# Attention in a hybrid block: queries loaded by tile, head loads spread, and one more quarter turned by DMA

## The reference, cut to what matters

```python
qf = jnp.transpose(qn.reshape(b, g, cq, h * w), (0, 1, 3, 2))
kf = jnp.transpose(key_.reshape(b, g, cq, h * w), (0, 1, 3, 2))
vf = jnp.transpose(value.reshape(b, g, cq, h * w), (0, 1, 3, 2))
scores = jnp.einsum('bgnc,bgmc->bgnm', qf, kf) * (1.0 / math.sqrt(c))
attn = jax.nn.softmax(scores, axis=-1)
ctx = jnp.einsum('bgnm,bgmc->bgnc', attn, vf)
```

## Time and profile before

| | |
|---|---|
| median of 3 runs | 8012.96 us |
| the profiled execution | 7983.15 us, span 7981.2 us |
| TensorE (PE), matmuls | 6932.5 us busy, 87% |
| VectorE (DVE) | 5846.9 us, 73% |
| GpSimd (POOL) | 5711.2 us, 72% |
| ScalarE (ACT) | 4440.0 us, 56% |
| DMA transposes `lo_turned<-p_lo`, issued by SP | 1024, 3.1 us from issue to landing (median) |
| loads of a head, issued by ScalarE | `q_head` 2 x 1024 KB, `k_head` 2 x 512 KB, `v` 1024 KB |
| store of a head, issued by ScalarE | `attn_out` 1024 KB |

### The profile page before, as it was taken

How to read it: one execution, slowest core, us unless ns; L and a number is a source line. 1 busy time by engine, 2 the same in 40 slices (tenths; PEclk the granted TensorE clock), 3 DMA queues, 4 the chain that set the end, 5 groups by cost and what they waited for, 6 DMA issues and landing times. The chain is left out here.

```text
span 7981.2 us, 140152 instructions
## 1 busy us (share of the span) xinstructions
PE 6932.5 (87%) x43076; PEld 4111.4 (52%) x43076; DVE 5846.9 (73%) x8015; ACT 4440.0 (56%) x7219; POOL 5711.2 (72%) x2792
## 2 busy tenths in 40 slices
PE   8798999899899759999999999999999986858992
PEld 6565666666566523443443444344444433536882
DVE  4486777787678648999899989989989996640116
ACT  2376777777677536656656665666566552212223
POOL 0187787787788529999999999999999995331006
PEclk9899999999999879999999999999999998978995
DMA  3467767767767641111211211121121112342113
GB/s 107 120 123 129 136 122 135 137 121 137 130 122 128 166 137 69 67 54 66 72 51 67 72 67 55 66 73 50 66 72 67 55 64 78 135 154 74 58 56 130
DMA packets 1256926, 755.82 MB, mean 95 GB/s; under 512 B 1113238, under 2 KB 1151796, under 8 KB 1235504
## 3 DMA queue, kind: packets, MB, share of 16 engines
q1 hardware_dynamic: 1233360, 677.46, 33.4%
q10 hardware_dynamic: 17120, 58.83, 2.9%
q0 software_dynamic: 6144, 16.33, 0.6%
HBM read 360.72 MB, written 123.73 MB: 61 GB/s over the span
## 5 line engine op out<-in xcount | busy, mean ns | idle before, releaser
L1492 DVE TENSOR_TENSOR_SCAN hh<-mb_ps_da,state,hh 128x512 f32<-128x512 f32 x2048 | 2496.0, 1273 | 126.4 <-POOL hh L1405 73.9
L1405 POOL TENSOR_TENSOR hh<-dtx,bb 128x1024 f32<-128x1024 f32 x1024 | 2399.6, 2369 | 214.6 <-PE mb_ps_y L1154 210.3
L661 POOL TENSOR_TENSOR p_lo<-prob 128x1024 bf16<-128x1024 f32 x1024 | 1906.8, 1893 | 803.1 <-ACT prob L612 664.6
L1295 ACT ACTIVATE mb_ps_da<-dt,amat 128x512 f32<-128x512 f32 x2048 | 1391.6, 686 | 1336.2 <-DVE hh L1492 1329.6
L1154 PE MATMUL mb_ps_y<-hh,ident 128*128 128x512 f32 x4096 | 1971.3, 609 | 17.4 <-POOL hh L1411 12.0
L676 DVE TENSOR_SCALAR_CACHE_REDUCE prob<-ps_s 128x1024 f32<-128x1024 f32 x1024 | 1213.8, 1223 | 487.5 <-PE ps_s L543 487.4
L1154 PEld LDWEIGHTS mb_ps_y<-hh,ident 128*128 128x128 f32 x4096 | 790.1, 195 | 962.5 <-issue 855.2
L612 ACT ACTIVATE prob<-prob,nmx 128x1024 f32<-128x1024 f32 x1024 | 1163.6, 1138 | 53.8 <-issue 19.5
L1499 DVE TENSOR_TENSOR hh<-hh,mb_ps_c 128x1024 f32<-128x1024 f32 x768 | 927.9, 1208 | 248.7 <-PE mb_ps_c L1143 214.6
L543 PE MATMUL ps_s<-k_head,q_tile 64*128 64x512 f32 x4096 | 1030.5, 622 | 46.2 <-ACT q_tile L648 45.8
L567 PE MATMUL ps_o<-v,hi_turned 128*128 128x128 bf16 x8192 | 841.0, 221 | 140.0 <-DMA lo_turned<-p_lo 138.6
(11 more groups left out here) (222 smaller groups left out, 8103.6 us busy)
## 6 DMA issues: line engine op xcount, KB each, us to landing
bb<-mb_bc SPq DMA_DIRECT2D x128, 1024.0 KB, 4.6
cc<-mb_bc SPq DMA_DIRECT2D x256, 256.0 KB, 3.1
lo_turned<-p_lo SPq DMA_TRANSPOSE x1024, 3.1
mb_u<-u SPq DMA_DIRECT2D x32, 512.0 KB, 3.2
m_dirs<-mo SPq DMA_DIRECT2D x32, 512.0 KB, 8.3
ex_w<-in_L_ffn_w SPq DMA_DIRECT2D x16, 1024.0 KB, 7.5
q_head<-q_full ACTq DMA_DIRECT2D x12, 1024.0 KB, 19.3
xbuf<-ml_zero SPq DMA_DIRECT2D x16, 640.0 KB, 5.5
```

The lines of the kernel that those rows point to most:

```text
L661: pool.tensor_tensor(lo[:, c, :], prob[s.u][:, cs], hi_view[s.u][:, 2 * c * PW + 1:2 * (c + 1) * PW:2], ALU.subtract).then_inc(lo_ready, 1)
L1295: act.activation(ps_da[:, exp_bank(e), :], dt[:, j, blk, :], ACT.Exp, scale=amat[:, j, blk, r % S:r % S + 1]).then_inc(da_ready, 1)
L1405: pool.tensor_tensor(hh[:, r % RING], dtx[:, j, half(r // S)], bb[:, r % S, :].unsqueeze(1).broadcast_to([P, HK, CH]), ALU.mult).then_inc( ...
L1492: dve.tensor_tensor_scan(h, a, h, state[:, s.j, q % S, blk:blk + 1], ALU.mult, ALU.add).then_inc(scanned, 1)
```

## The change

Four things change in attention.

1. Queries are no longer loaded a head at a time. SP loads the 128 queries of a tile straight from `q_full` into `q_tile`, in two loads of 64 rows x 512 bytes (32 KB), two tiles ahead. ScalarE's copy is gone.
2. The loads of keys and values are cut in halves and issued by ScalarE one at a time: keys in tiles 0 and 1, values in tiles 3 and 30; the store of the head before stands in tile 2. For that, tiles 0 to 3, 30 and 31 are written out.
3. Piece 3 of the upper halves is no longer turned by TensorE. ScalarE packs it into `p_hi` (128 x 1024 bfloat16), and SP issues a fifth DMA transpose for it, between those of pieces 1 and 2 of the lower halves.
4. Of the three pieces that are left, ScalarE evicts 1 and VectorE 0 and 2; the two PSUM buffers alternate over three pieces a tile.

Semaphores are split accordingly (`k_loaded`, `v_loaded`, `q_loaded`, `hi_ready`, `hi_turned`). The first scores wait for the keys and queries of head 0 alone, the first product of each head for its values.

The diff, cut to its core:

```diff
-    qf = [sb(f"q_head{j}", [P, L]) for j in range(2)]
+    hi = sb("p_hi", [P, PW], BF16)
...
-    ON_ACT, ON_DVE = (1, 2), (0, 3)
+    ON_ACT, ON_DVE, CROSSED = (1,), (0, 2), 3
...
         step(Tile(h, j, hp, 0, 0, opening, closing, first=True))
-        step(Tile(h, j, hp, 1, 1, opening, closing))
-        with eng.Fori(1, QT // 2 - 1) as it:
+        for t in range(1, 4):
+            step(Tile(h, j, hp, t, t % 2, opening, closing))
+        with eng.Fori(2, QT // 2 - 1) as it:
...
-        if k in ON_ACT:
+        if k == CROSSED:
+            eng.wait_ge(hi_turned, ONE + (g + 1) * 16)
+        elif k in ON_ACT:
...
+    def load_k(eng, h, j, half):
+        part = slice(DH * half, DH * half + DH)
+        eng.dma_start(kf[j][part], k_full[ds(h * DH, DH), :].rearrange("d (c two n) -> d two c n", two=2, n=CH)[:, half]).then_inc(k_loaded[j], 16)
+
+    def load_v(eng, h, j, half):
+        part = slice(half * QT // 2, (half + 1) * QT // 2)
+        eng.dma_start(vv[j][:, part, :].rearrange("p t c -> p (t c)"),
+                      v_split[h, :, half * L // 2:(half + 1) * L // 2]).then_inc(v_loaded[j], 16)
+
+    def load_q(eng, h, t, u):
         for half in range(2):
+            eng.dma_start(qcur[u][DH * half:DH * half + DH, :], q_full[ds(h * DH, DH), ds(t * P, P)]).then_inc(q_loaded[u], 16)
...
         def _(sp):
             def step(s):
+                if s.q_after:
+                    sp.wait_ge(s_ready, ONE + (s.g + 1) * PAIR)
+                    stand(sp, stood)
+                    load_q(sp, s.h + 1 if s.q_next_head else s.h, s.u if s.q_next_head else s.t + 2, s.u)
                 for c in range(PIECES):
...
                     sp.dma_start_transpose(lo_t[:, s.u, c], lo[:, c, :]).then_inc(lo_turned[c], 16)
+                    if c == 1:
+                        sp.wait_ge(pv_done, ONE + s.g * PIECES + 2 * PIECES)
+                        stand(sp, stood)
+                        sp.wait_ge(hi_ready, ONE + s.g + 1)
+                        stand(sp, stood)
+                        sp.dma_start_transpose(hi_t[:, CROSSED, :].rearrange("p (m c) -> p m c", c=P), hi[:, :]).then_inc(hi_turned, 16)
...
                 for k in range(PIECES):
-                    transposes(s, k)
+                    if k != CROSSED:
+                        transposes(s, k)
...
+            def pack(s):
+                act.wait_ge(exp_ready, ONE + (s.g + 1) * PIECES)
+                act.wait_ge(hi_turned, ONE + s.g * 16)
+                act.activation(hi[:, :], hi_view[s.u][:, 2 * CROSSED * PW + 1::2], ACT.Copy).then_inc(hi_ready, 1)
 
             def step(s):
                 exps(s.g, s.u, 3)
-                if s.q_after:
-                    tile_of(s)
                 turn(s, 1)
-                turn(s, 2)
+                pack(s)
...
-                if s.store_before:
-                    store(act, s.h - 1, 1 - s.j)
-                if s.load_after:
-                    load(act, s.h + 1, 1 - s.j)
+                if s.static and not s.opening:
+                    if s.t < 2 and not s.closing:
+                        load_k(act, s.h + 1, 1 - s.j, s.t)
+                    if s.t == 2:
+                        store(act, s.h - 1, 1 - s.j)
+                    if s.t == 3 and not s.closing:
+                        load_v(act, s.h + 1, 1 - s.j, 0)
+                    if s.t == QT - 2 and not s.closing:
+                        load_v(act, s.h + 1, 1 - s.j, 1)
```

More of the change, by code:

```diff
@@ L464, in attention_phase, with __init__ @@
     class Tile:
-        def __init__(s, h, j, hp, t, u, opening, closing, first=False, last=False):
+        def __init__(s, h, j, hp, t, u, opening, closing, first=False, last=False, pair=None):
             s.h, s.j, s.hp, s.t, s.u = h, j, hp, t, u
             s.g = h * QT + t
+            s.g2 = h * (QT // 2) + (t // 2 if pair is None else pair)
             s.before, s.after = not (first and opening), not (last and closing)
@@ L530, in step @@
                     sp.dma_start_transpose(lo_t[:, s.u, c], lo[:, c, :]).then_inc(lo_turned[c], 16)
-            load(sp, 0, 0)
-            load(sp, 1, 1)
+                    if c == 1:
[4 more added lines that the diff above has]
+                        sp.dma_start_transpose(hi_t[:, CROSSED, :].rearrange("p (m c) -> p m c", c=P), hi[:, :]).then_inc(hi_turned, 16)
+            load_q(sp, 0, 0, 0)
+            load_k(sp, 0, 0, 0)
+            load_k(sp, 0, 0, 1)
+            load_q(sp, 0, 1, 1)
+            load_v(sp, 0, 0, 0)
+            load_v(sp, 0, 0, 1)
+            for half in range(2):
+                load_k(sp, 1, 1, half)
+                load_v(sp, 1, 1, half)
             heads(sp, step)
@@ L548, in transposes, with values @@
                 pe.wait_ge(exp_ready, ONE + s.g * PIECES + k + 1)
-                turned(pe, s.g, k - 2)
+                slot = (s.u + k) % 2
+                if k == 2:
+                    turned(pe, s.g, 0)
+                else:
+                    turned(pe, s.g - 1, k + 1)
                 for m in range(BLOCKS):
                     at = 2 * (k * PW + m * P)
-                    last = pe.transpose(ps_t[:, k % 2, m * P:(m + 1) * P], hi_view[s.u][:, at + 1:at + 2 * P:2], ident16[:, :])
+                    last = pe.transpose(ps_t[:, slot, m * P:(m + 1) * P], hi_view[s.u][:, at + 1:at + 2 * P:2], ident16[:, :])
                 last.then_inc(t_ready, 1)
-            def values(hi=None, low=None):
+            def values(hi=None, low=None, first=False, hp=0):
                 if hi:
@@ L559, in values @@
                     turned(pe, g, k)
+                    if k == 0 and first:
+                        pe.wait_ge(v_loaded[j], ONE + (hp + 1) * 32)
                     if k == 0:
@@ L575, in step @@
                 for k in range(PIECES):
-                    transposes(s, k)
+                    if k != CROSSED:
+                        transposes(s, k)
                     if k >= LAG:
                         low = (s.g, s.u, s.j, k - LAG - 1) if k > LAG else (s.g - 1, 1 - s.u, s.jb, PIECES - 1) if s.before else None
-                        values((s.g, s.u, s.j, k - LAG), low)
+                        values((s.g, s.u, s.j, k - LAG), low, s.static and s.t == 0, s.hp)
                     elif s.before:
@@ L709, in step @@
                     maximum(s.g + 1, 1 - s.u)
-                turn(s, 3)
+                turn(s, 2)
                 if s.before:
```

54 lines of the change are left out of this document (19 added, 35 removed).

## The result

The changed kernel takes **8147.24 us** (median, 8140.28 to 8148.33) where the kernel before, measured beside it, takes 8012.81: a ratio of 1.0168, 95% interval 1.0151 to 1.0186. It is slower by 134 us. The forecast said slower by 43 us, 8056. Its sign and its bound were right, the size was a third of what came. The range held the time by 3 us (7915 to 8150), and the forecast's own ends, 7990 to 8145, missed it by 2.

What follows compares the result with a forecast made beforehand. SP's issue queue was to bound attention at 9.26 us a tile: +6 for tiles, +49 for head loads, -12 at the start, +43 us in sum, giving 8056 us against the median 8012.96; range 7915 to 8150.

Steps and rivals of the forecast that it cites:

- the forecast's own ends: Span of the main case, SP as the bound, from its terms' lower and upper ends: 7990 to 8145 us, chance 0.56.
- The bound: In attention, SP's issue queue becomes the bound at 9.26 us a tile, against 8.09 for TensorE and 7.45 for GpSimd.
- TensorE's part: In each attention tile TensorE loses eight transposes, 0.46 us, and alone would need 8.09 us instead of 8.55.
- ScalarE and VectorE, no term: Per tile the two swap similar work, staying near 6.8 and 6.9 us busy, so nothing was added to the forecast.
- SP's sum of 9.26 us a tile: SP's queue per tile: 6.26 today, 1.54 fifth transpose, 0.29 and 0.10 gaps, 1.07 two query loads; +6 us in all.
- 24 tiles with constant numbers, 0.8 us less each: Six tiles outside the loop in each of heads 0, 1, 6 and 7 have shorter gaps on SP, 0.8 us less each.
- Loads of a head, +49: At head changes, key and value loads and stores stretch SP's issues: 19 MB at 2.6 us each, +49 us.
- Start, -12: At attention's start, first scores need only four issues and two key loads, so begin earlier: -12 us (-5 to -18).
- The DMA engines keep up: In each tile, five transposes take 6.8 us of the DMA engines' time, out of 9.26, so they do not bound.
- TensorE stays the bound: Rival: SP's queue hides gaps and issues, its attention tile stays below 8.09 us; -238 us, 7775 us; chance 0.10.
- Cheap loads: Rival: each query load holds SP only 0.32 us, so SP needs 8.83 us a tile; 7946 us; chance 0.22.
- Query loads stretch the transposes: Rival: on SP's shared queue, query loads lengthen one of five transposes in every tile; +256 us, 8312 us; chance 0.12.

Runs made afterwards that it cites:

- early queries: The changed kernel with ScalarE issuing the query loads one tile earlier, and three SP waits a tile fewer; tiles 28 and 29 also written out: 7869.99 us.
- without the crossing: The changed kernel without its fifth transpose and packing: TensorE turns all four upper pieces, query loads by tile and spread head loads stay: 7868.62 us.

## Why the prediction was right or wrong

**The bound: right.** The prediction named SP's queue, with transposes and query loads end to end and all its waits early. The trace has 9.4 us of waits in 2500, and moving two issues to another queue gave 263 us.

**TensorE's part: nearly right.** It was to need 8.09 us a tile alone; where it is full in the presence of a crossing, the tile is 8.21.

**ScalarE and VectorE, no term: right.** Neither is full in any of the windows above, and in the whole of attention the packing waited for a crossing six times, 6.3 us in all:

```profile
  ACT p_hi L656: 6.3, 6
```

**SP's sum of 9.26 us a tile: too small, and this is the step that failed.** Each issue was priced well: two query loads with the gap between them at 1.07 + 0.10 us against 1.12 and 1.16 in the queue's rows, a transpose at 1.54 from start to start. What was mis-sized are the steps between issues, in three places.

Around the query loads the sum has 0.29 + 0.31 us; the queue's rows have 0.38 ahead of them and 0.35 behind (518.89 to 519.27 and 511.16 to 511.51). For the turn of the loop, "6.26 us SP is issuing four transposes and counting its registers" is four times 1.54 and 0.10, so it left 0.2 us every second tile. It takes 0.39 (9.66 against 9.27). If it took as long in the kernel before, a tile's steps came to 4 x 1.54 + 0.39 / 2 = 6.36 us there, an estimate, and 0.10 of them lay hidden in waits. The tile in which the loop does not turn takes 9.27, and that this meets the sum's 9.26 is luck: the sum has 0.10 for the turn in it, that tile none. The third place is the head: 9.27 and 9.66 hold for head 0. In the middle four heads, where the number of the head is a register too, tiles take up to 9.85 us, as here in head 4:

```profile
1748.16 1.11 SPq L523 DMA_DIRECT2D q_tile<-q_full  x2
...
1758.01 1.17 SPq L523 DMA_DIRECT2D q_tile<-q_full  x2
```

The mean tile is 9.62 to 9.64 us in these four heads, and 9.46, 9.56, 9.37 and 9.52 in heads 0, 1, 6 and 7; that the register makes the difference was not tested, and heads with constant numbers differ among themselves as much. Over all heads the mean tile is 9.56. That is 0.30 us above the sum, about a third of it from each place, 256 x 0.30 = 77 us, most of the 99 us by which attention grew beyond the forecast (154 against 6 + 49). The removal of three idle waits, 92 us, shows by itself that such steps have that size.

**24 tiles with constant numbers, 0.8 us less each: right where it can be seen.** 8.44 us stands against 9.27.

**Loads of a head, +49: the loads right, the rest too small.** At 2.6 us a MB the 12 MB of keys and values were to cost 31 us. Cutting their bytes gave 31 in the ledger and 30 in the time. The stores and the changes themselves were put at 18. In the span that the forecast counts, first exponential to last, what lies above 256 mean tiles is 2499.7 - 2446 = 54 us. That is what all of it costs less the 19 us saved by constant tiles, so 54 + 19 - 31 = 42 remain for them. That is 24 us more, which with the 77 makes up the 99; why was not tried apart.

**Start, -12: right**, 356.0 against 368.1. The wait for the first query tile, 45.8 us, became a wait of TensorE for the keys:

```profile
PE ps_s L569 <- DMA k_head<-k_full: 33.0, 1, 33.0
```

**The DMA engines keep up: right for the change.** Their share is 0.76 there, where the sum has 6.8 of 9.26 us, 0.73. Once SP was relieved it rose to 0.84 and 0.87, and head changes began to cost what the tiles gained; how much of that is the DMA engines' own doing stays open.

**The rivals.** "TensorE stays the bound", 7775, is what the kernel would be with SP's part gone and nothing in its place; even with early queries it came to 7870. The sentence of the Trainium skill behind it ("DMA: Bandwidth & Descriptors", "Issuing engines are not separate DMA queues": the time to initiate is "usually small relative to the DMA itself") is not borne out here: a query load's issue takes 0.524 us beside 2.1 to landing, a transpose's 1.232 beside 3.3. The same section's other statement, that transfers interleave on the same 16 DMA engines whoever issues them, is not shown by itself, but the runs agree with it: with the query loads on ScalarE's queue the DMA share rose from 0.76 to 0.84, where the same transfers in the shorter tile would give 0.76 x 9.56 / 8.42 = 0.86. "Cheap loads" fell by the row of 0.524 us. "Query loads stretch the transposes" fell too: a transpose takes 1.232 us at the median, as before.

## What to carry to other kernels

Before a DMA is added to a queue, add up that queue's tile as if it were an engine: every issue from start to start, each wait and register step even where it never waits, the turn of the loop, and the most general form of the addresses. A wait can hide such steps before the change, so price them from a stretch in which the queue runs without waits. And when one part of a change frees a bound, look at what the stage loses elsewhere before counting the gain: here 0.35 us a tile for TensorE, 89 us in all, cost 92 at the head changes (35 to 127), about half of it with the bytes of the head loads and about a third with TensorE's clock, two parts that overlap. The part that only rearranged loads kept all of its 140 us.

## What the runs showed of the hardware

- A 64-row load of 32 KB held its issuing queue for 0.524 us at the median, one of 32 rows and 16 KB for 0.361, on SP. Issued from ScalarE, the 64-row load had a median of 0.550. While ScalarE's queue issues, its computing goes on: in the run with the query loads on ScalarE the packing starts at 505.83 between two issues.

```profile
505.37 0.48 ACTq L523 DMA_DIRECT2D q_tile<-q_full  x1
505.83 1.04 ACT L652 ACTIVATE p_hi<-prob 128x1024 bf16<-128x1024 bf16 x1
505.93 0.56 ACTq L523 DMA_DIRECT2D q_tile<-q_full  x1
```

- The transpose of 128 x 1024 two-byte values held SP for 1.232 us at the median, before as after; beside the head loads the issue itself stretched, to 4.208 us at most in the change.
- Three satisfied waits with their register steps cost 0.40 us a tile on SP.
- TensorE's granted clock fell to the lower of its levels behind its idle time at head changes: for 85 us of attention with early queries and the crossing, for 10 us without the crossing.
